# A two-layer kernel on one core: its hand-written order of work is replaced by another, and a PSUM bank is released earlier

## The reference

```python
x = L0_attn_hidden_states                       # (4, 512, 128)
xn = _layernorm(x)
x = x + _L0_attn_ref(xn, ...) + _L0_ffn_ref(xn, ...)
xn = _layernorm(x)
x = x + _L1_attn_ref(xn, ...) + _L1_ffn_ref(xn, ...)
```

## Time and profile before

| | us |
|---|---|
| median of 3 runs (lowest, highest) | 296.53 (294.93, 298.2) |
| profiled execution | 297.9 |
| its span, from first to last instruction | 296.2 |

### The profile page before, as it was taken

The page is one execution under the profiler, slowest core; times in us unless marked ns, Lnnn a source line. Parts: engine busy times, 40 slices in busy tenths (PEclk is TensorE's granted clock), DMA queues, the critical chain, the costliest instruction groups (busy, mean ns, idle before and its releaser), DMA issues.

```text
span 296.2 us, 6413 instructions
## 1 busy us (share of the span) xinstructions
PE 261.4 (88%) x2185; PEld 166.1 (56%) x2185; DVE 185.4 (63%) x523; ACT 140.2 (47%) x231; POOL 78.7 (27%) x113
## 2 busy tenths in 40 slices
PE   7879997899899988999999999999998719399990
PEld 5434642355553544765343945445687719299990
DVE  4759519966852477655178676768597699733330
ACT  1582724755546145434652536562633415246660
POOL 3714800100000000340030040305105160088884
PEclk9989959999999999999999999999999987789997
DMA  6890099999940000000000010002431059688930
GB/s 167 206 310 7 3 240 167 186 252 168 207 144 0 2 1 2 9 29 0 2 0 0 2 30 0 11 2 62 108 91 30 9 136 250 187 192 205 205 27 2
DMA packets 40319, 27.04 MB, mean 91 GB/s; under 512 B 5088, under 2 KB 35856, under 8 KB 40288
## 3 DMA queue, kind: packets, MB, share of 16 engines
q1 hardware_dynamic: 37024, 24.51, 37.2%
q0 software_dynamic: 3264, 2.12, 4.2%
HBM read 13.43 MB, written 13.66 MB: 91 GB/s over the span
## 4 chain that ended last, share of the span: by engine, by line
PE 62%; DVE 18%; issue 9%; POOL 4%; ACT 3%; DMA 1%; POOLq 1%; DVEq 0%; ACTq 0%
PE SC L836 12%; PE WB L809 12%; PE YT L856 11%; PE WB L896 6%; PE WB L790 4%; POOL out_dram L655 4%; PE WB L876 2%; ACT A L696 2%; PE WB L803 1%; PE WB L885 1%; PE WB L821 1%; DVE X L1203 1%; PE WB L874 1%; DVE ATT L1201 1%; PE WB L932 1%
## 5 line engine op out<-in xcount | busy, mean ns | idle before, releaser
L696 ACT ACTIVATE A<-SC 128x2048 f32<-128x2048 f32 x40 | 75.1, 1877 | 59.4 <-PE SC L836 54.1
L836 PE MATMUL SC<-QM,KT 32*128 32x512 f32 (+1 forms) x384 | 46.3, 559 | 4.5 <-ACT A L696 4.5
L856 PE MATMUL YT<-A,VH 128*18 128x256 f32 (+1 forms) x768 | 43.0, 351 | 1.5 <-DVE A L1241 1.3
L1241 DVE SCALAR_TENSOR_TENSOR A<-A,TRI 128x1024 f32<-128x1024 f32 x32 | 38.1, 1218 | 6.9 <-ACT A L696 5.5
L523 POOL TENSOR_TENSOR RSTD<-VE,NHALF 128x2 f32<-128x2 f32 (+1 forms) x12 | 10.7, 893 | 96.1 <-DVE VE L1014 96.0
L604 POOL DMA_INDIRECT xs_dram<-XN,POS x16 | 17.5, 1092 | 63.7 <-DVE POS L1118 60.6
L655 POOL DMA_INDIRECT out_dram<-KT,ROW x18 | 27.9, 1551 | 21.6 <-DVE KT L1251 16.4
L856 PEld LDWEIGHTS YT<-A,VH 128*18 128x18 f32 x768 | 19.1, 98 | 25.6 <-issue 16.8
L836 PEld LDWEIGHTS SC<-QM,KT 32*128 32x128 f32 x384 | 16.6, 183 | 21.1 <-issue 16.4
L758 ACT ACTIVATE QM<-SC,B1T 128x128 f32<-128x128 f32 x72 | 20.6, 368 | 13.0 <-PE SC L973 8.9
L809 PE MATMUL WB<-XNT,WG 128*128 128x512 f32 x40 | 23.6, 674 | 0.2 <-DVE HT L1371 0.2
(11 more groups left out here) (246 smaller groups left out, 405.3 us busy)
## 6 DMA issues: line engine op xcount, KB each, us to landing
xs_dram<-INIT SPq DMA_DIRECT2D x1, 8775.0 KB, 47.2
W1S<-in_L_ffn_w_dram SPq DMA_DIRECT2D x16, 256.0 KB
HT<-in_L_ffn_w_dram SPq DMA_DIRECT2D x7, 256.0 KB
XSL<-xs_dram SPq DMA_DIRECT2D x23, 65.0 KB
X<-_attn_hidden_states_dram SPq DMA_DIRECT2D x4, 256.0 KB, 3.4
y_dram<-INIT SPq DMA_DIRECT2D x1, 1024.0 KB, 49.5
out_dram<-X SPq DMA_DIRECT2D x4, 256.0 KB, 2.4
HT<-y_dram SPq DMA_DIRECT2D x3, 256.0 KB, 4.0
```

What stands on the lines that cost most here:

```text
L696: act.activation(squares(n).rearrange("p k r c w -> p r k (c w)"), SC[:, :, 0:k * w].rearrange("p r (k w) -> p r k w", k=k), ACT.Square, b ...
L836: last = pe.matmul(SC[:, r, cols].rearrange("p (c w) -> p c w", w=width), KT[rows, b % 2, blk, i * P:(i + 1) * P], QM[rows, b % 2, blk, 0: ...
L856: last = pe.matmul(YT[QUAD * r:QUAD * r + 2 * VW, cols], VH[:, b % 3, i, NQ * blk + r, 2 * head:2 * head + 2], squares(n)[:, k, r, head], ...
L1241: dve.scalar_tensor_tensor(out=a, in0=a, scalar=1.0, in1=keep, op0=ALU.add, op1=ALU.mult).then_inc(masked, 1)
```

## The change

All 402 words of the plan are put in a new order and four words, `fi.0` to `fi.3`, are added. `late_slot(n)` does on DVE what the loop after the plan did for late slot n, and the loop begins at 4. The bank of a rank product is released by the operation that last reads it: the product with the choices for routes 0, 1 and 3, the reading of the counts for 2 and 4. The copy to `JUNK` is gone. Of the plan the diff shows the first lines.

```diff
@@ -53,6 +53,8 @@
 FIRST = 2
 SUMS_AT = 3
 SAVE_AT = 5
+IDS_AHEAD = 3
+PLANNED = 4
 RT_STEPS = 8
 
 RING_KINDS = ("xt", "q", "k", "v", "lg", "g", "u", "wt", "w", "of", "n", "at", "oa",
...
-ls.0 ln.0 xt.0 ls.1 q.0 k.0 ln.1 v.0 sq.0
-s.0 q.1 k.1 sq.1 mk.0 g.0 sq.2 mk.1
-s.1
...
+ls.0 ln.0 xt.0 ls.1 q.0 k.0 ln.1 v.0 ls.2
+s.0 q.1 ln.2 sq.0 k.1 g.0
+s.1 xt.1 u.0 sq.1 ls.3 mk.0 ln.3 g.1 k.2 sq.2 g.2
+s.2 xt.2 u.1 av.0
...
+fi.0 fi.1 fi.2 fi.3 ey.4
...
@@ -276,7 +278,6 @@
         SLOT = sb("SLOT", [1, LATE], I32)
         ESLOT = sb("ESLOT", [1, EARLY], I32)
         EPACK = sb("EPACK", [1, 1], I32)
-        JUNK = sb("JUNK", [P, 1])
         SPARE = sb("SPARE", [P, 1])
         SMX = sb("SMX", [P, TB * H])
         PROD = sb("PROD", [P, 2 * P])
@@ -1113,7 +1114,12 @@
                 wait_made(dve, ("rk", r))
                 q = PICK[:, lo:hi]
                 ranks = w[:, 0:(hi - lo) * E1].rearrange("p (t e) -> p t e", e=E1)
-                seq(dve.tensor_tensor(q, ranks, OH[:, lo:hi], ALU.mult))
+                ins = dve.tensor_tensor(q, ranks, OH[:, lo:hi], ALU.mult)
+                if r in (ER, NR - 1):
+                    seq(ins)
+                else:
+                    used(ins, ("rk", r))
+                    wait_used(dve, ("rk", r))
                 dve.wait_ge(scores_kept, r + 1)
                 dve.tensor_reduce(POS[:, lo:hi], q, AX.X, ALU.max).then_inc(pos_ready, 1)
 
@@ -1121,7 +1127,8 @@
 
                 lo, hi = ROUTES[ER]
                 counts = bank(("rk", ER))[0:1, (hi - lo) * E1:(hi - lo + 1) * E1]
-                seq(dve.tensor_tensor(CNTI[:], counts, EBASE[0:1], ALU.subtract))
+                used(dve.tensor_tensor(CNTI[:], counts, EBASE[0:1], ALU.subtract), ("rk", ER))
+                wait_used(dve, ("rk", ER))
                 seq(dve.tensor_scalar(CNTI[:], CNTI[:], P.bit_length() - 1, None, ALU.arith_shift_right))
                 seq(dve.tensor_copy(CNTF[:], CNTI[:]))
                 dve.scalar_tensor_tensor(out=STEPS[:], in0=CNTF[:], scalar=float(-E1 * P), in1=STEP[:], op0=ALU.mult, op1=ALU.add)
@@ -1156,8 +1163,9 @@
 
                 lo, hi = ROUTES[-1]
                 counts = bank(("rk", NR - 1))[0:1, (hi - lo) * E1:(hi - lo + 1) * E1]
-                seq(dve.scalar_tensor_tensor(out=CNTI[:], in0=counts, scalar=float(P - 1), in1=EBASE[0:1],
-                                             op0=ALU.add, op1=ALU.subtract))
+                used(dve.scalar_tensor_tensor(out=CNTI[:], in0=counts, scalar=float(P - 1), in1=EBASE[0:1],
+                                              op0=ALU.add, op1=ALU.subtract), ("rk", NR - 1))
+                wait_used(dve, ("rk", NR - 1))
                 seq(dve.tensor_scalar(CNTI[:], CNTI[:], P.bit_length() - 1, None, ALU.arith_shift_right))
                 seq(dve.tensor_copy(CNTF[:], CNTI[:]))
                 dve.wait_ge(late_bound, 1)
@@ -1259,6 +1267,12 @@
                 dve.tensor_tensor(YO[u], DOWN[n % 2], B2[:, bass.ds(e * D, D)], ALU.add).then_inc(y_summed, 1)
                 dve.wait_ge(y_summed, n + 1)
                 score(s)
+
+            def late_slot(n):
+
+                for k in range(0 if n == 0 else n + IDS_AHEAD, min(n + IDS_AHEAD + 1, LATE)):
+                    keep_ids(EARLY + k)
+                finish(n)
 
             for kind, n in plan:
                 item = (kind, n)
@@ -1314,7 +1328,6 @@
                         early_table()
                     if n == NR - 1:
                         slot_table()
-                    used(dve.tensor_copy(JUNK[:], PRI[:, 0:1]), item)
                 if kind == "q":
                     b, blk = divmod(n, NB)
                     wait_made(dve, item)
@@ -1340,6 +1353,8 @@
                     add_sums(n)
                 if kind == "ha":
                     add_heads(n)
+                if kind == "fi":
+                    late_slot(n)
                 if kind == "ew":
                     dve.wait_ge(early_ready, 2)
                     packed = dve.value_load(EPACK[0:1, 0:1], min_val=0, max_val=E1 ** EARLY - 1)
@@ -1404,13 +1419,8 @@
                         variances(2 * n, 2 * n + 2)
 
 
-            ahead = 3
-            for s in range(EARLY, EARLY + ahead):
-                keep_ids(s)
-            for n in range(LATE):
-                if n + ahead < LATE:
-                    keep_ids(EARLY + n + ahead)
-                finish(n)
+            for n in range(PLANNED, LATE):
+                late_slot(n)
 
 
 # ---- launch: one core; inputs and outputs as the reference has them ----
```

More of the change, by code:

```diff
@@ new lines @@
+s.0 q.1 ln.2 sq.0 k.1 g.0
+s.1 xt.1 u.0 sq.1 ls.3 mk.0 ln.3 g.1 k.2 sq.2 g.2
+s.2 xt.2 u.1 av.0
+s.3 xt.3 mk.1 mk.2 sq.3 g.3 u.2 lg.0 rt.0 q.2 u.3 sq.4 rt.1 k.3
+s.4 rt.2 av.1 ys.2 rt.3 av.2 rt.4 rt.5 g.4 g.5
+s.5 av.3 sq.5 av.4 u.4 u.5 g.6 cn.0
+s.6 rt.6 sq.6 rt.7 g.7 q.3 n.0
+s.7 wt.0 sq.7 av.5 av.6 w.0 sq.8 w.1
+s.8 u.6 mk.7 g.8 u.7 v.1 g.9 sq.9 mk.8 w.2 sq.10
+s.9 av.7 av.8 w.3 cw.0
+s.10 u.8 mk.9 q.4 g.10 mk.10 of.0 vp.0 ys.9
+s.11 av.9 at.0 vp.1 sq.11 of.1 q.5
+s.12 sq.12 oa.0 mk.11 k.4 rs.0 mk.12 v.2 n.1 k.5
@@ new lines @@
+s.13 av.10 av.11 sq.13 wt.1 av.12 ys.12 l2.0 at.1 cm.0 sq.14
+s.14 u.9 u.10 v.3 oa.1 sq.15 w.4
+s.15 x2.0 rs.1 g.11 av.13 l2.1 av.14 w.5
+s.16 x2.1 g.12 n.2 u.11 sq.16 g.13 xd.0 sq.17
+s.17 w.6 pd.0 w.7 av.15 mk.17 av.16 sq.18
+s.18 u.12 mk.18 g.14 xd.1 pd.1 mk.19
+s.19 of.2 ys.19 sq.19 sq.20
+s.20 av.17 av.18 av.19 at.2 u.13
+s.21 oa.2 mk.20 sq.21 g.15 mk.21 vp.2 u.14 mk.22
+s.22 n.3 sq.22 k.6
+s.23 av.20 sq.23 sq.24 av.21 rs.2 wt.2 av.22 l2.2 w.8 w.9
+s.24 at.3 ra.0 sq.25 ys.22 of.3
+s.25 q.6 es.0 q.7 u.15 sq.26
@@ new lines @@
+s.26 av.23 sq.27 av.24 wt.3 av.25 w.10 w.11
+s.27 g.16 rk.0 sx.0 w.12 sx.1
+s.28 x2.2 mk.27 u.16 oa.3 rs.3 sq.28 k.7 n.4 xd.2 sq.29 mk.28 w.13
+s.29 av.26 av.27 av.28 l2.3 x2.3 g.17 pd.2
+s.30 at.4 mk.29 of.4 xd.3 oa.4 sq.30 sq.31 ys.29 av.29 pd.3 rs.4
+s.31 u.17 n.5 g.18 sq.32 mk.30 mk.31 l2.4
+s.32 vp.3 at.5 mk.32 of.5 w.14
+s.33 sq.33 sx.2 sx.3 av.30 ra.1 sq.34 av.31 av.32 oa.5 es.1
+s.34 x2.4 rs.5 l2.5 ys.32 rk.1 u.18
+s.35 x2.5 sq.35 xd.4 pd.4 sx.4 g.19 n.6 xd.5
+s.36 sx.5 ra.2 sq.36 av.33 av.34 es.2 sx.6 pd.5 rk.2 w.15 sq.37
@@ L147 @@
+s.37 at.6 sx.7 u.19 av.35 av.36 tk.0 sq.38 sx.8
+s.38 mk.37 sx.9 mk.38 sq.39 sx.10 of.6
+s.39 sx.11 oa.6 mk.39 of.7 av.37 av.38 rs.6 av.39 et.0 l2.6 ys.39 x2.6 ew.0 et.1 n.7 xd.6 at.7 eu.0 pd.6 ra.3 oa.7 es.3
+rs.7 l2.7 eu.1 et.2 rk.3 ed.0 x2.7 hc.0 ed.1 et.3 xd.7 ra.4 eu.2 sx.12 ey.0 vb.0 pd.7 es.4 sx.13 rk.4 et.4 eu.3 ed.2
+eu.4 hc.1 ed.3 ed.4 hp.0 ha.0 ha.1 hp.1 ha.2 ey.1 sm.0 sx.14 sm.1 sx.15 ey.2 ha.3 sm.2 ha.4 ey.3 vb.1 ha.5 ha.6 ha.7
+fi.0 fi.1 fi.2 fi.3 ey.4
 """
```

12 lines of the change are left out of this document (removed).

## The result

| | kernel before | changed kernel |
|---|---|---|
| median, us | 297.37 (294.93 to 300.06, 4 runs) | 275.88 (274.04 to 277.37, 4 runs) |
| ratio of the runs | | 0.93, 95% interval 0.92 to 0.94 |
| profiled execution | 297.9, span 296.2 | 275.12, span 273.4 |

A forecast was written before the change was run, and what follows sets the result against it. Up to 212 us, PE's work plus 15.4 us of holes and half clock bounds the kernel. 5.8 + 3.0 + 1.6 + 1.1 - 0.2 = 11.3 us of gain gave 285.5 us, range 279.5 to 295.5.

The forecast's parts named there:

- Step 1: Up to 63 us: less PE idle time and half clock, gain 5.8 us, bounds 0.4 and 9.8.
- Step 2: From there to the last score product: 4.9 us idle, 1.9 left for DVE waits, gain 3.0 us.
- 3, work moved behind s.39: `oa.6` and `av.37` no longer stand before s.39, which starts 1.6 us earlier.
- Step 4: From s.39 to the last route's positions: 23.0 us for 24.1, gain 1.1 us, bounds -1.5 and 2.
- Step 5: Behind the positions: slot 4's output later, residual sums, stores and 18 scatters not shortened, loss 0.2 us.
- Step 6: `fi` words where the loop had them, earlier bank release for routes 0 to 3 hidden or counted elsewhere: 0 us.
- the rival without it: No half clock at the gate product, as dense products stand around it: 282.2 us, chance 0.17.
- the possibility that prices hide slack: PE's product prices hide slack, so short fillers were worth only the shown waits: 295 us, chance 0.10.
- My count of short intervals (6.5 us): Eight places between old-plan score products with under 2.16 us of PE filler, together 6.5 us short.
- a sign of being wrong: The prediction is wrong if the tail behind the positions grows by more than 1 us.
- value sums holding banks: In DVE's in-order queue, eight `ys` copies hold banks PE needs, 2.3 us each: 303.6 us, chance 0.11 for slower.
- DVE as the bound: Bunched DVE work reopens holes in places, first two parts give 1 to 4 us: some 291.5 us, chance 0.12.

The follow-up runs named there:

- old_release: The kernel before, old order of work, with only the rank products' banks released early; 298.46 us, ratio 0.9994 to the kernel before.
- thin6: Changed kernel with one piece of PE filler moved out of six intervals behind the next score product; 278.57 us, ratio 0.9393 to the kernel before.
- experiment 4: Old order with filler moved behind s.1, score products moved behind filler, or squarings moved behind their products; ratios 1.000 to 1.040 to the kernel before.
- hold_last: Changed kernel with only the last route's bank held by the extra copy as in the old kernel; 278.32 us, ratio 0.9367 to the kernel before.
- new_hold: Changed kernel's new order with the old release, the copy to `JUNK` freeing the banks; 281.11 us, ratio 0.9475 to the kernel before.

## Why the prediction was wrong, step by step

| step | predicted gain | measured, less the gate clock |
|---|---|---|
| 1, up to s.9 (now s.8) | 5.8 | about 8.4 |
| 2, to s.39 | 3.0 | about 10.1 |
| 3, work moved behind s.39 | 1.6 | 1.6 (taken as predicted) |
| 4, s.39 to the positions | 1.1 | 1.3 |
| 5, behind the positions | -0.2 | -0.9 to -2.3 |
| 6, release and `fi` words | 0 | 0 in the old order, 2.4 to 5 in the new one, within the rows above |

The measured column: old_release has s.9 at 59.85 and s.39 at 208.53, the changed kernel s.8 at 51.63 and s.39 at 188.43. That is 8.2 and 11.9 us. Up to s.8 the new order has `u.5`, `g.6`, `g.7` and `n.0` done and not yet s.8, `v.1`, `w.2`, `w.3` and `av.7`: 3.7 us by starts for 3.5, so 0.2 us more; and 1.6 us is moved. Behind the positions stood 60.1 us of span before, and 62.4, 61.3 and 61.0 in three profiles after.

1. **Step 1, mis-sized.** s.2 starts at 20.76 without a wait, as said, and the inputs came in time. The 1.7 us for the clock behind the hole was right. Wrong were the 0.7 us for a late s.1 and the 1.0 us of waits on the experts' weights that I left: s.1 starts at 15.67 and PE has no gap at all. Some 1.4 us more came as less busy time, as in step 2: 42.79 us in old_release, of which some 1.7 for the clock, and 39.81 now. The slow stretch that I kept for the gate product is a matter of the execution, not of the order: my 3.0 us and the rival without it each describe some executions. The Trainium skill ("TensorE: Matmul & The Clock Gate", Part 1) has the clock follow how busy PE is; that fits the clock behind the hole, which full fillers removed, and doesn't fit 32:36 above, where equally busy executions got 1.00 and 0.60.
2. **Step 2, the one that failed.** I took the 4.9 us of idle rows as all that could be gained there, and left 1.9 of it; what PE's busy time could give stood in the sum at nothing. Both were wrong. Only 0.8 us of idle remained. And PE's busy time fell from 144.16 to 136.01, of which 1.8 is work that lies elsewhere now: some 6.3 us are the same work in less busy time. The traces show three parts of it; the sizes are estimates.
   - Ends of products ahead of a wait, as in thin6. By its shares (1.3 busy for 3.2 idle) the old order's 4.9 us of idle hid up to 2 us.
   - Value products in a row. One alone costs 0.99 us by starts (94.53 to 95.52). In the changed kernel two take 1.85 and three 2.71:

```profile
39.72 1.92 PE L857 MATMUL YT<-A,VH 128*18 128x256 f32 x32
41.57 1.98 PE L810 MATMUL WB<-XNT,WU 128*128 128x512 f32 x4
...
145.25 2.79 PE L857 MATMUL YT<-A,VH 128*18 128x256 f32 x48
147.96 0.44 PE L913 MATMUL WB<-IDF,XN 128*128 128x128 f32 x2
```

   The old plan has the 30 value products of this stretch in 29 places, the new one in 16: some 2 us.
   - Products of 512 columns. Beside their own kind they cost 0.86 us, behind a score or value product 0.96; the old order has them more often so: 0.95 us on average there (old_release), 0.92 in the changed kernel, some 0.9 us.

   The remaining 1.4 us or so are open, and no run changed only what stands beside what. My prices (0.86, 0.99) were right for one neighbourhood each; I had taken them for all. I had named the possibility that prices hide slack, but as a reason for less gain; it was one for more. My count of short intervals (6.5 us) was no list of repairs either, as experiment 4 showed.
3. **Step 4 and the last positions** came nearly as worked out (22.8 us to their end for 23.0), but the working hid how much the new tail is needed: with the old tail the same front takes 27.3.
4. **Step 5** was too small: in the first profile a down product waits 1.4 us for ACT, and a sum 1.02 us for its load, and the tail grew by 2.3 us, more than the 1 us that I had named as a sign of being wrong; in the two later profiles it grew by 0.9 and 1.2. The 18 scatters at 1.87 us apart are as predicted.
5. **Step 6, wrong for the release.** I compared it with the old order, where it is in truth worth nothing (0.9994), and checked in the new one only what stands behind `rk.2`. Behind the last route the next down product stands on the held bank for 2.5 to 3.0 us, and slot 4's chain behind it: from the last positions to the end hold_last takes 64.6 us and new_hold 64.7, the changed kernel 61.0 to 62.4.

The rivals: value sums holding banks did not come (DVE's waits for their products are 1.1 us for 2.3, and PE never waited for one); DVE as the bound did not come either. The good ends of all terms, 279 us, were still 3 us above the result, because that of step 2 was bounded by idle rows.

## What to carry to other kernels

In this kernel idle rows were a lower bound of what an order loses: compare the busy time of an engine for the same instructions between stretches, count the intervals that lack filler, and take a product's price from the neighbours that it will have. Don't expect that a hole can be filled by itself: the move must be made on every queue that serves it, and the next engine's order (here DVE's `ln` behind its masks) can be what stood behind the hole. And cost a released buffer in the order in which it will be used, not in the one that it comes from.

## What the runs showed that I had not expected

The half clock at the gate product comes and goes between executions of one kernel at the same place, with PE equally busy, and costs 1.7 or 3.2 us of 294 (the groups of times above). With the product cut into three parts it came in one profile too. What decides it is open. And a product's time by starts depends on what stands beside it, by 0.1 us of 0.9.
